# A two-layer graph network on one core: layer 0 written out pair by pair, with the spectra of the taps made four pairs later

## The reference

```python
# layer 0
norm  = (sum(adj, -1) + 1e-6) ** -0.5
f_hom = (adj @ ((x @ theta) * norm)) * norm
f_het = x @ W_h
gate  = sigmoid(x @ W_t + b_t)
x     = layernorm(x + elu(gate * f_hom + (1 - gate) * f_het))
# layer 1: a 1x1 and a 17-tap convolution over the nodes, batch norms,
# message passing over exp(-distance), a GRU cell, a residual and a layernorm
```

## Time and profile before

| | |
|---|---|
| median of three runs | 2074.39 us (2072.35 to 2077.55) |
| the profiled execution | 2074.34 us, its span 2072.6 us |
| `phase_a` | 0 to 543.0 us of the span |
| the other three phases | 543.0 to 2072.6 us, 1529.6 us |
| PE busy in the span | 92% |
| DMA in the span | 263.23 MB, 127 GB/s |

### The profile page before, as it was taken

How to read it: one execution, slowest core, us unless ns; L and a number is a source line. 1 busy time by engine, 2 the same in 40 slices (tenths; PEclk the granted TensorE clock), 3 DMA queues, 4 the chain that set the end, 5 groups by cost and what they waited for, 6 DMA issues and landing times.

```text
span 2072.6 us, 36523 instructions
## 1 busy us (share of the span) xinstructions
PE 1900.2 (92%) x11046; PEld 1662.2 (80%) x11046; DVE 1508.9 (73%) x2960; ACT 1149.6 (55%) x2174; POOL 509.2 (25%) x438
## 2 busy tenths in 40 slices
PE   6888888888599979994999999999999999999997
PEld 5777778787499968883788888888888888888886
DVE  5999899799466666764777777777777777777774
ACT  6887788688366666663444444444444444444442
POOL 5887678587344400000000000000000000000000
PEclk9999999899799989996899999999999999999998
DMA  4655666565533277885122121212121221212110
GB/s 139 211 203 197 215 218 214 177 214 195 179 98 101 81 232 252 266 257 184 51 83 79 65 91 51 95 47 95 47 95 65 78 85 58 95 47 95 65 42 21
DMA packets 175099, 263.23 MB, mean 127 GB/s; under 512 B 13406, under 2 KB 125764, under 8 KB 170788
## 3 DMA queue, kind: packets, MB, share of 16 engines
q1 hardware_dynamic: 175012, 262.27, 37.6%
HBM read 174.14 MB, written 88.08 MB: 127 GB/s over the span
## 4 chain that ended last, share of the span: by engine, by line
PE 51%; issue 1%; DVE 1%; DMA 1%; SPq 0%; ACT 0%; POOLq 0%; POOL 0%; ACTq 0%; DVEq 0%
PE c_ps_g L1440 38%; PE c_ps_m L1418 4%; PE c_ps_m L1449 2%; PE c_ps_y L1475 1%; PE c_ps_m L1451 1%; PE c_ps_y L1533 1%; PE c_ps_m L1533 1%; PE c_ps_m L1450 1%; DMA c_yf<-y_spec 1%; PE c_ps_s L1518 0%; PE c_ps_y L1534 0%; PE c_ps_m L1534 0%; PE c_ps_s L1489 0%; PE c_ps_g L1492 0%; DVE c_wi_l L1383 0%
## 5 line engine op out<-in xcount | busy, mean ns | idle before, releaser
L1209 POOL TENSOR_TENSOR c_rstd<-c_var_eps,c_neg_half 128x4 f32<-128x4 f32 x32 | 32.2, 1007 | 1078.3 <-DVE c_var_eps L1347 1078.3
L1132 ACT ACTIVATE c_yo<-c_ps_y,c_shift,c_rstd 128x256 f32<-128x256 f32 x128 | 61.8, 563 | 169.5 <-DVE c_shift L1355 169.5
L1440 PE MATMUL c_ps_g<-c_ch,c_wi_l 128*128 128x512 f32 x384 | 154.4, 402 | 0.0
L1440 PE MATMUL c_ps_g<-c_nh,c_wi_l 128*128 128x512 f32 x384 | 153.2, 399 | 0.0
L1440 PE MATMUL c_ps_g<-c_xh,c_wh_l 128*128 128x512 f32 x384 | 152.2, 396 | 0.0
L1440 PE MATMUL c_ps_g<-c_xl,c_wh_h 128*128 128x512 f32 x384 | 152.1, 396 | 0.0
L1440 PE MATMUL c_ps_g<-c_xh,c_wh_h 128*128 128x512 f32 x384 | 151.6, 395 | 0.0
L1440 PE MATMUL c_ps_g<-c_ch,c_wi_h 128*128 128x512 f32 x384 | 151.6, 395 | 0.0
L1440 PE MATMUL c_ps_g<-c_cl,c_wi_h 128*128 128x512 f32 x384 | 151.5, 394 | 0.0
L839 PE MATMUL m_ps<-m_wh,m_xl 128*128 128x256 f32 (+1 forms) x406 | 132.6, 327 | 20.3 <-DVE m_wl L819 20.2
L1440 PE MATMUL c_ps_g<-c_nl,c_wi_h 128*128 128x512 f32 x384 | 151.1, 394 | 0.0
(11 more groups left out here) (225 smaller groups left out, 6426.3 us busy)
## 6 DMA issues: line engine op xcount, KB each, us to landing
w_spec<-a_spec SPq DMA_DIRECT2D x32, 1088.0 KB, 11.1
m_w<-w_spec SPq DMA_DIRECT2D x34, 1024.0 KB, 7.7
a_xt<-in_x_t SPq DMA_DIRECT2D x64, 256.0 KB
a_xn<-in_x_n SPq DMA_DIRECT2D x64, 256.0 KB, 9.4
x_t<-a_x1t SPq DMA_DIRECT2D x64, 256.0 KB, 9.7
s_x<-x_t SPq DMA_DIRECT2D x64, 256.0 KB, 3.0
y_spec<-m_y SPq DMA_DIRECT2D x64, 256.0 KB, 5.6
c_x<-x_t SPq DMA_DIRECT2D x32, 512.0 KB, 4.2
```

Source lines behind the costliest of these rows:

```text
L1132: nc.scalar.activation(yo[:, b], ps_y[:, b], ACT.Identity, bias=shift[:, b:b + 1], scale=rstd[:, b:b + 1]).then_inc(s_yo, 1)
L1440: last = nc.tensor.matmul(out, stationary, moving, start=(count == 0), stop=(count == total - 1))
```

## The change

`phase_a` gets a helper `written_out`, which writes all 71 steps (77 on SP) in a row, without a loop. Beside that:

- The taps go another way. Every fourth step SP loads a batch of four pairs' taps into 128 rows (`tr`, 272 KB); ACT rounds it (`th`), DVE subtracts (`tl`), and SP stores high, low and high to HBM (`taps_s`, three transfers of 272 KB). From there each pair's 102 rows are loaded by one transfer (`gs`, 204 KB, a ring of four). `gr`, `gh` and the DVE step L407 are gone.
- The spectra of a pair are made at steps i + 6 and i + 7 instead of i + 2, and the orders in a step are new. PE: degree, projection 0, spectrum 3 (of pair i - 7), `ps_hom`, spectrum 0 (of pair i - 6), projection 1, spectrum 1, transposition, gate (waits for `gd`, not for `gate`), spectrum 2. ACT: below, exp, `xh`, copy 3, `ah`, `fh` 0, copy 0, [`th`], `fh` 1, `het`, copy 1, `x1t`, gate, copy 2. DVE: degree + eps, `y`, bn_stats, bn_aggr, `diff`, variance + eps, `gd`, `mix`, `x1`, `fl`, [`tl`]. POOL: `roots`, `xl`, `res`, `al`. What stands in brackets comes every fourth step. The blocks of spectra are stored five steps later (`piece = n % 8 - 1`), the last one after the last `x1t`.
- The two powers of POOL are one of four columns (`roots`); `var_eps` is made by DVE and not by ACT.
- The gate stays in PSUM (tanh in place), and `gd` and `mix` read PSUM where they read SBUF.
- `x1` is a scalar_tensor_tensor with a broadcast second input where it was a tensor_scalar.
- `xn` has four buffers where it had two.

```diff
+def written_out(units, stages, step, unroll):
+    for i in range(units + stages - 1):
+        step(i, i % unroll, i // unroll, lambda s, i=i: 0 <= i - s < units)
...
+    TB = 4
+    TC = 2 * TAPS * TB * 4 * P // P
...
-        gr = sb("gr", [ROWS, RING, 4, P])
-        gh = sb("gh", [ROWS, 4, P], F32R)
-        gs = sb("gs", [ROWS, 2, 4, P], F32R)
+        tr = sb("tr", [P, TC])
+        th = sb("th", [P, TC], F32R)
+        tl = sb("tl", [P, TC], F32R)
+        gs = sb("gs", [ROWS, RING, 4, P], F32R)
...
@@ SP @@
-                    reached(sp, s_gs, i - RING + 1)
-                    for copy in range(3):
-                        sp.dma_start(gr[copy * 2 * TAPS:(copy + 1) * 2 * TAPS, r].rearrange("p c k -> p (c k)"),
-                                     taps[:, bass.ts(i, 4 * P)]).then_inc(s_in[r], 16)
+                    if n % TB == 0:
+                        reached(sp, s_tl, m)
+                        sp.dma_start(tr[:, :], here.rearrange("o p c -> (o p) c")).then_inc(s_tr, 16)
                 if live(4):
...
+                    if n % TB == 0:
+                        m = k * (UNROLL // TB) + n // TB - 1
+                        reached(sp, s_tl, m + 1)
+                        for copy, part in enumerate((th, tl, th)):
+                            sp.dma_start(here[:, copy].rearrange("o (p c) -> (o p) c", p=P), part[:, :].bitcast(F32)).then_inc(s_ts, 16)
+                if live(6):
+                    reached(sp, s_ts, 48 * (m + 1))
+                    sp.dma_start(gs[:, r].rearrange("p c k -> p (c k)").bitcast(F32),
+                                 here.rearrange("o h (r x c) -> (o h r) x c", x=TB, c=4 * P)[:, at_step]).then_inc(s_gs[r], 16)
-                piece = n % 8 - 4
-                if 0 <= piece < PIECES and live(5 + piece):
+                piece = n % 8 - 1
+                if 0 <= piece < PIECES and live(10 + piece):
...
@@ ACT @@
-                    nc.scalar.activation(var_eps[:, :], mv[:, v, :, 1], ACT.Identity, bias=eps[:, 0:1]).then_inc(s_ve, 1)
-                    nc.scalar.activation(gate[:, u], ps_g[:, :, :], ACT.Tanh, scale=0.5).then_inc(s_gate, 1)
+                    nc.scalar.activation(ps_g[:, :, :], ps_g[:, :, :], ACT.Tanh, scale=0.5).then_inc(s_gate, 1)
...
@@ POOL @@
-                    nc.gpsimd.tensor_tensor(norm[:, u], deg_eps[:, :], neg_half[:, :], ALU.pow).then_inc(s_norm, 1)
-                    nc.gpsimd.tensor_tensor(rstd[:, v], var_eps[:, :], neg_half[:, :], ALU.pow).then_inc(s_rstd, 1)
+                    nc.gpsimd.tensor_tensor(roots[:, u, these], sums_eps[:, u, these], neg_half[:, these], ALU.pow).then_inc(s_root, 1)
...
@@ DVE @@
+                    reached(dve, s_root, p5 + 3)
+                    nc.vector.scalar_tensor_tensor(sums_eps[:, v, 2:4], mv[:, v, :, 1], 1.0, eps[:, :], ALU.mult, ALU.add).then_inc(s_ve, 1)
-                    nc.vector.scalar_tensor_tensor(gd[:, :, :], gate[:, v], 1.0, diff[:, :, :], ALU.add, ALU.mult).then_inc(s_gd, 1)
+                    nc.vector.scalar_tensor_tensor(gd[:, :, :], ps_g[:, :, :], 1.0, diff[:, :, :], ALU.add, ALU.mult).then_inc(s_gd, 1)
-                    nc.vector.scalar_tensor_tensor(mix[:, v], gd[:, :, :], 0.5, het[:, v],
+                    nc.vector.scalar_tensor_tensor(mix[:, v], gd[:, :, :], 0.5, ps_hh[:, 2 * v:2 * v + 2, D:2 * D],
-                        last = nc.vector.tensor_scalar(x1[:, u, b], y[:, u, b], mv[:, u, b, 0:1], rstd[:, u, b:b + 1],
-                                                       ALU.subtract, ALU.mult)
+                        last = nc.vector.scalar_tensor_tensor(x1[:, u, b], y[:, u, b], mv[:, u, b, 0:1], roots[:, u, 2 + b:3 + b].to_broadcast([P, D]),
+                                                              ALU.subtract, ALU.mult)
-                    nc.vector.scalar_tensor_tensor(gs[:, v], gh[:, :, :].bitcast(F32), mk[0:ROWS, 2:3], gr[:, (n - 1) % RING],
+                    nc.vector.tensor_tensor(tl[:, :], tr[:, :], th[:, :].bitcast(F32), ALU.subtract).then_inc(s_tl, 1)
...
@@ PE @@
-                    reached(pe, s_gate, p2)
+                    reached(pe, s_gd, p2)
```

More of the change, by code:

```diff
@@ L130, in phase_a @@
         s_wl = sem("weights_low")
-        s_in = [sem(f"x_adj_taps_loaded{b}") for b in range(RING)]
-        s_xn = [sem("x_nodes_loaded0"), sem("x_nodes_loaded1")]
+        s_in = [sem(f"x_adj_loaded{b}") for b in range(RING)]
+        s_xn = [sem(f"x_nodes_loaded{b}") for b in range(RING)]
         s_xh = sem("x_high")
@@ L364, in step @@
                     nc.vector.scalar_tensor_tensor(y[:, v], mix[:, v], 0.0, res[:, v], ALU.max, ALU.add).then_inc(s_y, 1)
-                if live(3):
-                    reached(dve, s_gd, p3)
-                    reached(dve, s_hom, p3 + 1)
-                    reached(dve, s_het, p3 + 1)
-                    for b in range(2):
-                        last = nc.vector.scalar_tensor_tensor(diff[:, b], ps_hom[:, b], norm[:, v, b:b + 1], het[:, v, b],
-                                                              ALU.mult, ALU.subtract)
-                    last.then_inc(s_diff, 1)
-                if live(5):
                     reached(dve, s_mv, p5)
@@ L390, in step @@
                 if live(3):
+                    reached(dve, s_gd, p3)
+                    reached(dve, s_hom, p3 + 1)
+                    reached(dve, s_het, p3 + 1)
+                    for b in range(2):
+                        last = nc.vector.scalar_tensor_tensor(diff[:, b], ps_hom[:, b], roots[:, v, b:b + 1], het[:, v, b],
+                                                              ALU.mult, ALU.subtract)
+                    last.then_inc(s_diff, 1)
+                if live(5):
+                    reached(dve, s_mv, p5 + 1)
+                    reached(dve, s_root, p5 + 3)
+                    nc.vector.scalar_tensor_tensor(sums_eps[:, v, 2:4], mv[:, v, :, 1], 1.0, eps[:, :], ALU.mult, ALU.add).then_inc(s_ve, 1)
@@ L429, in step, with spectra @@
                 terms = [(xx, ww, c) for c in range(KD) for xx, ww in ((xl, w_hi), (xh, w_lo), (xh, w_hi))]
-                def spectra(c):
+                def spectra(q, c, back):
+                    r = (n - back) % RING
                     if c == 0:
-                        reached(pe, s_gs, p2 + 1)
-                    reached(pe, s_gw, 4 * p2 + c)
-                    nc.tensor.matmul(ps_w[:, 0:GW], gs[:, u, c], dw[:, :], start=True, stop=True).then_inc(s_gm, 1)
+                        reached(pe, s_gs[r], 16 * (k * (UNROLL // RING) + (n - back) // RING + 1))
+                    reached(pe, s_gw, 4 * q + c)
+                    nc.tensor.matmul(ps_w[:, 0:GW], gs[:, r, c], dw[:, :], start=True, stop=True).then_inc(s_gm, 1)
                 def project(b):
@@ L454, in step @@
                     last.then_inc(s_deg, 1)
+                    project(0)
+                if live(7):
+                    spectra(i - 7, 3, 7)
                 if live(3):
@@ L486, in step @@
                     last.then_inc(s_gp, 1)
-                    spectra(3)
-            pipeline(pe, pairs, STAGES, step, unroll=UNROLL)
+                if live(6):
+                    spectra(i - 6, 2, 6)
+            written_out(pairs, STAGES, step, UNROLL)
 def phase_spectrum(nc, G, x1_t, w_c1, bn1, masks, dft_f, x_spec):
```

182 lines of the change are left out of this document (94 added, 88 removed).

## The result

The changed kernel takes 2029.6 us in the median of 4 runs (2028.71 to 2030.04); the kernel before takes 2074.13 beside it. The ratio is 0.9783, with a 95% interval of 0.9766 to 0.98: 44.5 us faster. The forecast was 2018.0 with a range of 2000 to 2040, so the time lies 11.6 us above it and inside the range.

A forecast was written before the change was run, and what follows sets the result against it. It took DVE's whole list, then `ps_hom` on PE, to bound the step, plus stalls. Steps -64.6, start -2.6, drain +2 and tail +8.7 make -56.5: from 2074.3 to 2018 us, range 2000 to 2040.

The forecast's parts named there:

- rival A: The forecast itself: the ACT-PE circle sets the step at 6.8 to 7.0 us; 2012 to 2025 us, chance 0.58.
- (c): Circle between ACT and PE through the single buffer `ps_w`, copy 3, spectrum 0 and the gate: 6.88 us a step.
- (d): `gd` must end before the gate's matmuls: 1.7 us on DVE behind `ps_hom` against 2.0 on PE.
- (a): DVE's list of work in a step: from 7.08 us busy to 5.6 to 6.6.
- rival B: DVE stays the bound, as `x1` and the variance meet POOL: 7.2 to 7.4 us a step, 2037 to 2050, chance 0.14.
- (b): PE's own work in a step, less its idle time and a cold `ps_hom`: floor 6.5 to 6.7 us.
- rival C: PE's floor sets the step at 6.5 to 6.7 us, the circle not closing: 1993 to 2006 us, chance 0.10.
- rival E: `gs` load no faster than three `gr`, 4.4 us, so the queue sets 8.6 a step: 2125 us, chance 0.04.
- Rival D: The DMA queue sets the pace, `gs` at 3 us: about 7.2 us a step, 2037 us, chance 0.12.
- The jumps: Loop jumps at steps 32 and 48: the 20.4 us of stalls go, less what was late stores.
- The drain: Last six steps of `phase_a`, with four nearly hidden rounds of spectrum and copy in four of them: +2 us.
- The tail: End of `phase_a`: last block's four pieces stored behind the last `x1t`, 13 us where the gap was 4.35: +8.7 us.

The follow-up runs named there:

- e7: The changed kernel with DVE's variance + eps moved behind `mix`, so `gd` needn't wait for `xl`: 2030.69 us.
- e8: The changed kernel with two edits, ACT's copy 3 ahead of `xh` and DVE's variance + eps behind `mix`: 2017.47 us.
- e1: The changed kernel with ACT's copy 3 moved ahead of `xh`: 2026.46 us.
- e5: The changed kernel with `x1` put back from a scalar_tensor_tensor to a tensor_scalar: 2029.58 us.
- e4: The changed kernel with each `gs` load split into three transfers of 34 rows, the same bytes: 2126.22 us.
- e2: The kernel before, only with its steps written out without a loop: 2067.59 us.
- e9: The kernel before with its loop, but `gr` loaded by one transfer of 102 rows in place of three: 2050.84 us.
- e10: The kernel before with both edits, one `gr` load and no loop: 2044.35 us.
- e3: The changed kernel with the loop put back on all five engines: 2042.41 us.
- e6: The changed kernel with a pair's taps and spectra three steps sooner and the pieces stored four steps sooner: 2017.2 us.

## Why the prediction was right, and where it was off

The mechanism of rival A holds: the circle of ACT and PE sets the step, as the trace of the kernel after and `e7` with `e8` show. The forecast sum put the span at 2016.1 (2072.6 - 56.5); it is 2027.4. The 11.3 us between them are the table's differences less its forecasts: 4.8 in the steps, 1.7 at the start, 5.7 in the drain and 0.6 in the gap, less 1.5 in the other phases. The range of 2000 to 2040 is wide enough for this, but rival A's own, 2012 to 2025, is missed by 4.6 us.

**(c), the pace.** ACT's part was 2.9 and is 2.89; PE's was 3.90 and is 3.98; the signal back to ACT was 0.04 and is 0.04. The signal from ACT to a PE that stands idle was taken as 0.04 and is 0.15. That and PE's 0.08 behind it make 7.06 of 6.88. Every fourth step with `th` and `tl` is 0.4 longer and the next is shorter by as much, so a group of four has 7.05 on average; the whole, with short first steps, has 6.99. That the steps as a whole are only 4.8 us over is in part luck: 0.15 more in each of 63 is 9.5, and it is set off by first steps that were 3.5 us short for the 2 put, and by the 3 us for leftover waits that didn't come.

**(d), the wait that "fits by 0.3".** It did fit in the kernel after: four waits, and 0.5 us to spare in the step shown. What I had left out is POOL. The variance took 0.15 in my sum, and it takes 0.3 to 0.75 us, because it ends only with `xl`; so what `gd` waits for is not `ps_hom` but ACT's `xh` and then POOL's `xl`. My expectation for `e1` didn't work out that path, though it named a later `xh` as a risk of 0.3 us: the edit took 0.52 us out of the first circle and put 0.42 into the second, which then closed at 7.02. The expectation for `e8`, two circles of 7.05 and 7.02 in one kernel, is wrong in the same way; the 7.02 is a length that `e1` had made. The gain of both edits together stands.

**(a), DVE, and rival B.** DVE's list is 25.20 / 4 = 6.3 us busy a step, inside 5.6 to 6.6. `mix` fell to 0.69 as put. `x1` came between the ends, at 1.29 for 1.70. It costs nothing here (`e5`), with either form. The rule of the Trainium skill (SBUF — State Buffer, "SBUF: two separate sides"), that DVE with two SBUF inputs and POOL exclude each other, agrees with the variance's 0.32 and 0.75 us beside `xl` and 0.15 alone; it was right about the instruction, and in the kernel after the order of the engines made it harmless; in `e1` it wasn't. In `e8`, where both circles are short, DVE's list is near to being the bound: in the step shown it runs from 302.31 to 309.01 without idle time, 6.70 us. So is PE, busy for 6.70 us of the same stretch; that is the upper end of PE's floor in (b) and rival C, 6.5 to 6.7. Which of the two sets the 6.82 isn't shown.

**The DMA.** One `gs` was taken at a third of three `gr`; `e4` shows that the whole change hangs on it. The time that rival E had for a slow `gs`, 2125, was met by 2126.22 in `e4`. The waits for the `x1t` store went, and no wait for `gs` came. Rival D did not occur. Two sums of the prediction are off without a consequence: the bytes of a step are 1644 and 1916 KB, not 1648 and 1926, and a step with a piece of spectra and a whole batch of taps has 2.1 + 2.6 + 1.5 + 2.6 = 8.8 us of DMA, not 6.9; such steps are followed by lighter ones.

**The jumps.** "The 20.4 us go" came out right, since the loads and the jumps went together; the owner was left half open (both of ACT's "issue" waits stand at the jumps, "less what of them was the late stores"). The runs show that neither owns it alone. In the same seven steps the loop's removal takes 13.5 of the 20.4 us (`e2`) and the single load 15.8 (`e9`, 4.6 left). But in the whole phase the loop alone is worth only 6 us in the kernel before, since the full SP queue stops ACT elsewhere instead; the single load is worth 25, both 32 (`e10`). In the kernel after, the loop would cost 12.8 us (`e3`).

**The start.** PE starts at 15.69, not 14.0. `bt_rows` is the last constant, and POOL's `xl` and `al`, which start sooner now, run beside DVE while it makes the constants: `dw` takes 1.50 us here, until just behind the end of `xl` (13.65 and 13.36), and 0.50 in the kernel before. `bt_rows` then ends at 15.64. The timeline of all engines after:

```profile
11.17 2.19 POOL L348 TENSOR_TENSOR a_xl<-a_xt,a_xh 128x512 fp32r<-128x512 f32 x1 [9.47 <-ACT a_xh L284]
...
12.15 1.50 DVE L370 SCALAR_TENSOR_TENSOR a_dw<-a_dw_hi,a_mk,a_dw_raw 102x272 fp32r<-102x272 f32 x1
...
15.69 0.37 PE L478 MATMUL a_ps_t<-a_ones,a_al 128*128 128x2 f32 x1 [15.69 <-DVE a_bt_rows L376]
```

**The drain** is the term that was most mis-sized: +7.7 for +2. I took a round of spectrum and copy at 0.75 to 0.82 us, from steps in which PE is busy, and took the rounds as nearly hidden. With only `x1t` and spectra left nothing hides them. PE stands idle in each round, its granted clock from 464 to 485.6 is 0.57 on average (1.00 until 467, from there on 0.50, the level of 1.2 GHz), and a round takes 1.08 to 1.15 us. ACT in the kernel after:

```profile
476.02 0.40 ACT L268 ACTIVATE a_spec<-a_ps_w 128x272 f32<-128x272 f32 x1 [0.75 <-PE a_ps_w L461]
477.10 0.40 ACT L268 ACTIVATE a_spec<-a_ps_w 128x272 f32<-128x272 f32 x1 [0.68 <-PE a_ps_w L461]
477.96 0.60 ACT L311 ACTIVATE a_x1t<-a_ps_t 128x512 f32<-128x512 f32 x1 [0.45 <-PE a_ps_t L506]
```

Four rounds and an `x1t` make 4.66 us a step (473.30 to 477.96 for two `x1t`), where a step of the drain took 3.4 before. The low clock is only a part of it. A round at the granted clock of 1.00 already takes 0.92 us here (465.48 to 466.40) and 0.93 and 0.89 in `e6`, and the kernel before had the low clock in its drain too (0.78 on average, 0.50 from 530 on).

**The tail** was right: 13.6 us for 13, with the DMA engines 0.96 busy at 393 GB/s and every other engine idle. `e6` gives back 6.9 of it and 6.6 of the drain, with a granted clock of 0.78 in its window, as in the drain before. It changes the rounds in the drain and the clock at once, so how much each of the two costs isn't shown exactly.

## What to carry to other kernels

Before an instruction is moved out of one circle, look at what it then stands in front of: copy 3 left the circle that set the step and delayed, over `xh`, POOL and a two-column instruction on DVE, another one by nearly as much. Only with a second edit did the first one pay. Before a loop's jump is blamed for a stall, look for a queue that runs late at the same place, and for a transfer over few rows that holds it: one load in place of three was worth 25 us, the loop 6. Work that is moved to the end of a phase is paid at the prices of an idle machine, with nothing to hide behind and for the most part half the clock: 17 us here, of which 12 came back when it was moved forward again.

## What was not expected of the hardware

- A PE that waits for a signal from ACT starts 0.15 us behind it (304.69 to 304.84), where ACT starts 0.04 behind PE (308.82 to 308.86).
- What a taken jump costs depends on the transfers beside it, but not simply on how busy the DMA engines are: ACT stood for 4.5 us in the kernel before (0.34 and 0.49 busy), 4.0 in `e3` (0.82 and 0.90) and 2.2 in `e9` (0.82 and 0.87), whose one edit is the load.
- Two inputs in SBUF can cost even an instruction on two columns 0.6 us when POOL works: the variance took 0.75 us for 0.15 in `e1`, and ended within 0.03 us of POOL's `xl` in 60 of 64 steps.
